# A four-step turn of the attention result on TensorE against one block transpose on VectorE, with one rectification in sixteen on ScalarE

## The reference

```python
x = x + attn(xn) + moe(xn)
# attn: 8 heads, 2 channels each for queries and keys, 16 for values
scores = einsum("bmhd,bnhd->bhmn", q, k) / sqrt(2)
scores = where(scores >= 0, scores, 0.2 * scores)
beta = softmax(scores)
out = gamma * einsum("bhmn,bnhd->bmhd", beta, v) + xn
# moe: 16 experts (1 zero, 1 copy, 2 constant, 12 MLP of 128 -> 512 -> 128), top 2, capacity 1024 slots each
```

## Time and profile before

| | us |
|---|---|
| median of 3 runs (976.41 to 978.05) | 977.33 |
| the profiled execution | 976.61 |
| its span | 974.8 |
| DVE, L1030, 512 rectifications | 610.7 busy, 1.229 each |
| ACT, L636, 512 exponentials | 523.3 busy, 1.024 each |
| ACT, L628, 32 copies of the result | 18.6 busy, 0.580 each |
| DVE, L1016 and L1011, 32 each | 13.3 and 7.9 busy |
| POOL, L400, 32 additions | 23.5 busy, 0.735 each |

### The profile page before, as it was taken

How to read it: one execution, slowest core, us unless ns; L and a number is a source line. 1 busy time by engine, 2 the same in 40 slices (tenths; PEclk the granted TensorE clock), 3 DMA queues, 4 the chain that set the end, 5 groups by cost and what they waited for, 6 DMA issues and landing times.

```text
span 974.8 us, 19803 instructions
## 1 busy us (share of the span) xinstructions
PE 883.5 (91%) x7619; PEld 365.8 (38%) x7620; DVE 744.3 (76%) x851; ACT 716.5 (74%) x859; POOL 581.7 (60%) x574
## 2 busy tenths in 40 slices
PE   0688249999999999999999989999999999999997
PEld 0444102333333333867767723333333333333332
DVE  6698889999999995001011089999999999999996
ACT  0689878888888887454454468888888888888886
POOL 3355137776676662999999015647566574665770
PEclk9999659999999999999999989999999999999999
DMA  8723100101100011242342210010011002002100
GB/s 228 269 65 72 31 27 30 44 30 36 39 25 28 18 52 58 68 135 92 110 135 78 80 43 26 22 49 20 26 32 39 23 21 64 24 13 62 31 7 22
DMA packets 48163, 55.34 MB, mean 57 GB/s; under 512 B 10714, under 2 KB 35122, under 8 KB 48080
## 3 DMA queue, kind: packets, MB, share of 16 engines
q1 hardware_dynamic: 38464, 44.10, 14.8%
q0 software_dynamic: 8192, 9.37, 3.3%
q10 hardware_dynamic: 1424, 0.76, 0.3%
HBM read 31.58 MB, written 30.02 MB: 63 GB/s over the span
## 4 chain that ended last, share of the span: by engine, by line
PE 77%; ACT 9%; DVE 6%; issue 4%; DMA 1%; SPq 1%; POOLq 0%; ACTq 0%; DVEq 0%
PE ps L765 26%; PE ps L745 15%; PE ps L735 13%; PE ps L825 8%; PE ps L817 8%; ACT pr L636 4%; PE ps L775 3%; ACT ot L628 2%; DVE xn L897 1%; SPq L248 1%; PE ps L695 1%; PE ps L806 1%; ACT y L614 1%; DMA y<-in_x 1%; ACT va L592 1%
## 5 line engine op out<-in xcount | busy, mean ns | idle before, releaser
L1030 DVE TENSOR_SCALAR ps<-ps 128x1024 f32<-128x1024 f32 x512 | 610.7, 1229 | 20.9 <-PE ps L735 6.6
L636 ACT ACTIVATE pr<-ps 128x1024 f32<-128x1024 f32 x512 | 523.3, 1024 | 111.5 <-PE ps L745 101.0
L765 PE MATMUL ps<-pr,vp 128*32 128x256 f32 x4096 | 327.7, 392 | 0.3
L745 PE MATMUL ps<-q,kz 64*128 64x512 bf16 x1024 | 201.7, 391 | 9.2 <-DVE ps L1030 9.1
L735 PE MATMUL ps<-q,kz 62*128 62x512 bf16 x1024 | 199.9, 387 | 7.7 <-DMA q<-parts_dram 1.7
L445 POOL DMA_INDIRECT xs<-eout,idxs x128 | 129.0, 1008 | 108.7 <-ACT pr L636 78.5
L430 POOL DMA_INDIRECT disp<-xn,idx x128 | 125.6, 981 | 47.1 <-issue 35.8
L1042 DVE TENSOR_TENSOR pr<-ps,parts 128x1024 f32<-128x1024 f32 x12 | 14.7, 1225 | 166.1 <-PE ps L825 166.1
L745 PEld LDWEIGHTS ps<-q,kz 64*128 64x128 bf16 x1024 | 49.2, 93 | 222.0 <-DVE ps L1030 117.2
L765 PEld LDWEIGHTS ps<-pr,vp 128*32 128x32 f32 x4096 | 81.2, 108 | 108.1 <-issue 91.3
L663 ACT ACTIVATE pr<-ps,b1s 128x512 f32<-128x512 f32 x96 | 66.0, 687 | 48.8 <-PE ps L817 48.8
(11 more groups left out here) (120 smaller groups left out, 618.6 us busy)
## 6 DMA issues: line engine op xcount, KB each, us to landing
disp<-pr SPq DMA_DIRECT2D x12, 512.0 KB, 4.9
eout<-pr SPq DMA_DIRECT2D x12, 512.0 KB, 2.9
y<-in_x SPq DMA_DIRECT2D x8, 512.0 KB, 8.2
out<-y SPq DMA_DIRECT2D x8, 512.0 KB
w<-in_w1t SPq DMA_DIRECT2D x12, 256.0 KB, 3.1
w<-in_w2t SPq DMA_DIRECT2D x12, 256.0 KB, 3.3
xs<-disp SPq DMA_DIRECT2D x6, 512.0 KB, 4.8
pr<-disp SPq DMA_DIRECT2D x6, 512.0 KB, 4.8
```

The costliest lines, as they stand in the source:

```text
L636: act.activation(pr[:, c % BUFS, 2 * pair:2 * pair + 2, :], ring[i % RING], ACT.Exp, scale=SLOPE).then_inc(S["exps"], 1)
L745: last = pe.matmul(ring[i % RING][:, k, :], kz[r:r + TILE, hg, pair, kc * P:(kc + 1) * P], q2[r:r + TILE, hg, qh * HALF:(qh + 1) * HALF], ...
L765: last = pe.matmul(acc[p % 2][32 * g:32 * g + 32, cols], vp[:, hg, kc, g, :], pr[:, c % BUFS, g % PAIRS * 2 + g // PAIRS, cols], start=(kc ...
L1030: dve.tensor_scalar(s, s, 0.0, 1.0 / SLOPE - 1.0, ALU.max, ALU.mult).then_inc(S["relu"], 1)
```

## The change

The result of a pass is no longer turned by PE. DVE transposes `acc` into `ot` by one instruction, which transposes each 32 x 32 block on its own. Since each head has a band of 32 partitions, afterwards partition 32g + r holds, for head g, the queries whose number modulo 32 is r, 16 of them, each with 16 values and its denominator in 32 columns. DVE then takes the reciprocal from SBUF. The product moves to POOL (`quotient`), and its result `att` still has heads on partition bands, so SP moves it by 16 DMAs per pass (`spread`) into `moved`, where each partition is one token, and POOL adds that to `y`. Each DMA has 32 partitions x 4 runs of 64 bytes.

In addition unit 9 of every pass is rectified by ACT (`rectify`), in place in PSUM, between exponentials 7 and 8.

```diff
-EVAC = 4
-TURN = 6
-DENOM = 12
-FINISH = 13
+TURN = 5
+PARTS = 1
+BLOCK = 32
+BY_ACT = 9
...
@@ SP
+            def spread(p):
+                sp.wait_ge(S["att_rdy"], p + 1)
+                wait_done(sp, "y_att", p - 1)
+                for g in range(HG):
+                    rows = att[BLOCK * g:BLOCK * g + BLOCK, p % 2, :, :].rearrange("q (t r) d -> q t r d", r=P // BLOCK)
+                    for r in range(P // BLOCK):
+                        sp.dma_start(moved[BLOCK * r:BLOCK * r + BLOCK, p % 2, :, g, :], rows[:, :, r, :]
+                                     ).then_inc(S[f"spread{p % 2}"], 16)
...
+            for p in range(BH * NPB):
+                operands_in(p)
+                if p > 1:
+                    spread(p - 2)
...
             sp.wait_ge(S["pv"], BH * NPB * TB)
+            spread(BH * NPB - 2)
             load_expert(1, 1)
+            spread(BH * NPB - 1)
...
+            spread(B * NPB - 1)
+            store_sequence(B - 1)
@@ POOL
+            def quotient(p):
+                pool.wait_ge(S["rg_rdy"], p + 1)
+                wait_done(pool, f"spread{p % 2}", 16 * HG * GT * (p // 2))
+                rows = ot[:, p % 2, :].rearrange("p (q c) -> p q c", c=BLOCK)
+                pool.tensor_tensor(att[:, p % 2, :, :], rows[:, :, 0:DV],
+                                   rg[:, p % 2, :].unsqueeze(2).broadcast_to([P, HALF // BLOCK, DV]), ALU.mult
+                                   ).then_inc(S["att_rdy"], 1)
...
@@ ACT
-            def evacuate(p):
-                act.wait_ge(S["pv"], TB * (p + 1))
-                wait_done(act, "o_rdy", p - 1)
-                act.copy(ot[:, p % 2, :], acc[p % 2]).then_inc(S["acc_evac"], 1)
+            def rectify(i):
+                act.wait_ge(S["s1"], i + 1)
+                s = ring[i % RING]
+                act.activation(s, s, ACT.Relu, scale=1.0 / SLOPE - 1.0).then_inc(S["relu_act"], 1)
...
+                    if (i + 1) % UP == BY_ACT:
+                        rectify(i + 1)
                     exponentials(i)
@@ PE
-                    if 0 <= i % UP - TURN < GT and i > first + UP:
-                        turn(i // UP - 1, i % UP - TURN)
...
-                for t in range(GT):
-                    turn(end // UP - 1, t)
...
                     if n == 2:
-                        pe.wait_ge(S["att_rdy"], NPB * BH)
+                        pe.wait_ge(S["turned"], NPB * BH)
@@ DVE
+            def turn(p, part):
+                if part == 0:
+                    dve.wait_ge(S["pv"], TB * (p + 1))
+                    wait_done(dve, "att_rdy", p - 1)
+                cols = slice(part * HALF // PARTS, (part + 1) * HALF // PARTS)
+                last = dve.transpose(ot[:, p % 2, cols], acc[p % 2][:, cols])
+                if part == PARTS - 1:
+                    last.then_inc(S["turned"], 1)
...
+                    if 0 <= i % UP - TURN < PARTS and i > first + UP:
+                        turn(i // UP - 1, i % UP - TURN)
+                    if i % UP == TURN + PARTS and i > first + UP:
+                        denominators(i // UP - 1)
+                    if i % UP == BY_ACT:
+                        continue
```

More of the change, by code:

```diff
@@ L199, in build @@
                  "qz_init weighted gate_rdy row_step route max_rdy off_rdy reset_rdy r_exp cnt_rdy pos_rdy ztile init_rdy kz_init "
-                 "ld0 ld1 vp_rdy s1 relu s2 exps pv acc_evac o_rdy rg_rdy att_rdy y_att "
+                 "ld0 ld1 vp_rdy s1 relu relu_act s2 exps pv turned rg_rdy att_rdy spread0 spread1 y_att "
                  "scat staged pool_step carry "
@@ L309, in store_sequence, with operands_in @@
                              y[:, bass.ts(s, TB), :]).then_inc(S["final"], 16)
[L312 to L315, removed]
+            def spread(p):
[6 more added lines that the diff above has]
+                                     ).then_inc(S[f"spread{p % 2}"], 16)
+            def operands_in(p):
+                if p % NPB == 0 and p > 0:
+                    load_operands(p // NPB, 1)
+                if p % NPB == NQ and p // NPB + 1 < B:
+                    load_operands(p // NPB + 1, 0)
+            for hg in range(NHG):
+                load_operands(0, hg)
+            for p in range(BH * NPB):
+                operands_in(p)
+                if p > 1:
+                    spread(p - 2)
             sp.wait_ge(S["scat"], 16 * GS)
@@ L341, in _ @@
                 store_expert(E_MLP - 2 + u)
[L343 to L349, removed]
+            for p in range(BH * NPB, B * NPB):
+                operands_in(p)
+                if p > BH * NPB + 1:
+                    spread(p - 2)
+                if p % NPB == 0 and p > BH * NPB:
+                    for s in STORES[p // NPB - BH - 1]:
+                        store_sequence(s)
+            spread(B * NPB - 2)
+            for s in STORES[B - BH - 1][:-1]:
                 store_sequence(s)
+            spread(B * NPB - 1)
+            store_sequence(B - 1)
             sp.wait_ge(S["final"], 16 * B)
@@ L741, in shifted @@
                 p, hg, qh, kc, pair = unit_of(i)
-                pe.wait_ge(S["relu"], i + 1)
+                if i % UP == BY_ACT:
+                    pe.wait_ge(S["relu_act"], i // UP + 1)
+                else:
+                    pe.wait_ge(S["relu"], i + 1 - (i + UP - BY_ACT) // UP)
                 for k in range(2):
@@ L761, in values @@
                     pe.wait_ge(S["vp_rdy"], p // NQ + 1)
-                    wait_done(pe, "att_rdy", p - 1)
+                    wait_done(pe, "turned", p - 1)
                 for g in range(HG):
@@ L1022, in attention @@
                 for i in range(first, end):
-                    done = i // UP - 1 if i > first + UP else None
-                    if done is not None and i % UP == DENOM:
-                        denominators(done)
-                    if done is not None and i % UP == FINISH:
-                        finish(done)
+                    if 0 <= i % UP - TURN < PARTS and i > first + UP:
+                        turn(i // UP - 1, i % UP - TURN)
+                    if i % UP == TURN + PARTS and i > first + UP:
+                        denominators(i // UP - 1)
+                    if i % UP == BY_ACT:
+                        continue
                     dve.wait_ge(S["s1"], i + 1)
@@ L1030, in attention @@
                     dve.tensor_scalar(s, s, 0.0, 1.0 / SLOPE - 1.0, ALU.max, ALU.mult).then_inc(S["relu"], 1)
+                for part in range(PARTS):
+                    turn(end // UP - 1, part)
                 denominators(end // UP - 1)
-                finish(end // UP - 1)
             attention(0, BH)
```

46 lines of the change are left out of this document (18 added, 28 removed).

## The result

The changed kernel takes 1000.15 us (median of 4 runs, 998.95 to 1000.82) against 977.68 before in the same series: a ratio of 1.023, 95% interval 1.0215 to 1.0247. It is slower by 22.5 us. The forecast was 986.1, slower by 8.8, with a range that ended at 1004. The sign was right, the time lies inside the range, and the size was off by more than a factor of two.

The account below looks back on a forecast made before the run. The prediction took a TensorE and ScalarE loop of 1.20 us a unit as the bound. Passes +1.8, between stages -0.9 and tail +7.9 sum to +8.8: 985.4 from 976.6 profiled, median 986.1, range 978 to 1004.

Parts of the forecast that it names:

- The bound: Kernel before: a loop of 1.20 us a unit through TensorE and ScalarE, not VectorE, sets the pace.
- ScalarE's rectification: In the loop, between exponentials 7 and 8: exponential 8 starts 0.55 to 0.73 us late, taken as 0.60.
- VectorE's lateness: At unit 6 of a pass: VectorE, with transpose and reciprocal, needs 4.36 us where 4.12 is due, 0.24 late.
- Sum +0.02: A pass: -0.82 us for removed transposes and copy, +0.24 on VectorE, +0.60 on ScalarE; times 30 is +0.6.
- Rival 1: In a pass, the block transpose costs as 1024 columns, 0.77 us late in place of 0.24: +16, 1002; chance 0.18.
- rival 2: VectorE was the bound, so a pass drops 0.83 us: 959, or about 968 with ScalarE's 0.60 half hidden; chance 0.12.
- rival 4: In a pass, transpose 0.33 and ScalarE 0.55 make -0.27 us; -1.4 in all, no tellable change; chance 0.06.
- the price of an issue: SyncE's 16 transfers of a pass: 0.35 us each to issue plus 0.04 between two, 6.2 us in all.
- +7.9: Tail at the kernel's end: 14.55 us in place of 6.6, including fifteen issues of 0.39 (5.85).
- -0.9: Between the stages: -1.2 us as the experts start at once, +0.3 for the later load of expert 1.
- Cover: In the passes: SyncE's transfers have a whole pass to run beside; if that is gone, everything paces at SP.
- Rival 3: SP paces the passes: at 1.86 us an issue, 16 are 30 us a pass, adding over 300 us; chance 0.02.

Follow-up runs that it names:

- e1: The changed kernel with unit 9 rectified by VectorE again, so ScalarE runs only exponentials: 982.5 us, 1.0065 of the kernel before.
- e13: The kernel of e10 with the reciprocal taken before rectification 13 in place of 6, run in a second series: 963.5 us, 0.987 of the kernel before.
- e4: The changed kernel with each partition's 256 bytes moved in one run in place of four of 64, values landing in wrong places: 997.8 us.
- e9: The changed kernel with the product sent to DRAM by one transfer first and the 16 transfers per pass reading from there: 1010.7 us.
- e10: The changed kernel without ScalarE's rectification, the product moved through DRAM by five transfers in place of 16: 964.6 us, 0.987 of the kernel before.
- e5: The changed kernel with ten of the last result's 16 transfers issued by ScalarE and six by SyncE: 994.6 us, 1.0177 of the kernel before.
- e3: The changed kernel with SyncE's list between the stages reordered, the load of expert 1 first: 990.5 us.

## Why the prediction was right or wrong

**The bound was right.** A loop of 2.40 us for two units through TensorE and ScalarE. e1 shows it from one side (VectorE takes a sixteenth rectification and the pass gets shorter), and the 0.55 us of idle TensorE behind exponential 8 from the other.

**The terms of a pass were right.** Transpose 0.60 to the next start, measured 0.63. ScalarE's rectification 0.60, measured 0.58. VectorE's lateness 0.24, of which e1 leaves 0.2 over the bare loop and the pass shown above 0.23. Sum +0.02, measured -0.02. How VectorE's 0.24 was split, 0.60 from the transpose and 0.23 from the reciprocal against one slack, isn't borne out: e13 has the same passes without the 0.23. Rival 1, a transpose at the price of 1024 columns, is out, and so are rival 2, VectorE as the bound (its sum has a slip: 18.65 to 17.8 is 0.85, not 0.83), and rival 4, a pass 0.27 shorter.

**The rule on relu.** The Trainium skill, "ScalarE: Activation LUTs", rules for kernel authors, says to put it on VectorE, for speed per element, and its figure is for bf16. For this shape in four-byte values in PSUM that reason doesn't hold: 1.02 us on ScalarE (the L668 row) against 1.23 on VectorE. Its advice does, for another reason: ScalarE's operations are in the loop that sets the pace, and e1, with the rectification on VectorE, has passes 0.58 shorter.

**The step that failed is the price of an issue: "A transfer of 128 short runs (b1s, 16 bytes each) takes 0.35 to issue; I add 0.04 between two, so 16 take 6.2 us".** It measured 0.60 and 0.64, so 16 take 10.2, and 10.7 and 11.2 at the two ends. I chose a row by its number of runs, and e4 shows that this doesn't set the price. The trace of before had a row with both ends in SBUF, the eight small transfers into `kz` at the start, and I had not read it:

```profile
L256 SPq DMA_DIRECT2D kz<-rowones x8: 577/589/1617, 15.7 to 21.3; - x8
```

0.589, close to what was measured. That both have their ends in SBUF doesn't explain it, since e9 pays 0.599 from DRAM; but a price of 0.6 for a small transfer stood in the trace, as did the 0.624 of the second weight load (256 KB). The spread around the forecast took an issue to 0.45 at most, so the error was in the bounds too.

**It entered three times.** In the tail, fifteen steps of 0.68 in place of 0.39 are +4.3. Also in the tail, the last result's transfers stand behind those of the one before, 3.8 us (978.74 to 982.52). The prediction called the tail "laid bare" and began the issues at once. By its own price that would have held: the 32 issues from 960.16, at 0.39 each, end at about 973 (an estimate), before the product is ready. So this wait comes from the price too. Together with landings 0.4 shorter, +7.9 became +15.4. Between the stages the load of expert 1 went out at 394.4 in place of 389.0. That is 5.9 us of stall for which I had written 0.3, and then half the clock for some 6 us, which I had no term for: -0.9 became +7.5. POOL's rounds, which I had ending about 14 us later, ended 23.7 later (559.4), still beside the experts.

**Cover held where I named it.** Inside the passes the spread takes up half of SyncE's time (10.3 of 20 us) and the passes came out level. Rival 3, SyncE pacing the passes, was out by a factor of two.

## What to carry to other kernels

A step that is moved off the busy engines onto a queue is free only while something runs beside it. Work out the last one, and the one at each change of stage, as a bare sum, with all that the queue still has to issue ahead of it. Where no row is known to fit, bound the price of a DMA issue by the cheapest and the dearest row of small transfers (in the trace of before 0.25 and 0.59 us), not by the one that looks alike. Count the issues before the bytes: here five transfers by way of DRAM were cheaper than sixteen within SBUF. Before work is passed from the busiest engine to another, ask which of the two lies in the loop that sets the pace.

## What the runs showed of the hardware that was not expected

- An issue on SyncE cost 0.59 to 0.60 us for pieces of 8 KB in four forms (32 partitions by four runs of 64 bytes, from SBUF or from DRAM; 32 by 256 bytes; 128 by 64 bytes), 0.63 for 32 KB from SBUF to DRAM (e10), and 0.33 to 0.35 for 128 KB over 128 partitions in one run each. On ScalarE's queue the median was 0.622, against 0.601 on SyncE's for the same piece (e5). Two loads of one form cost 0.333 and 0.624, the second issued right behind the first.
- A block transpose of 128x512 four-byte values from PSUM takes VectorE 0.71 us, 0.63 to the next start, between its 256-column (0.33) and 1024-column operations (1.13).
- ScalarE rectifies 128x1024 in place in PSUM in 1.02 us, as long as it takes for an exponential into SBUF.
- After 5.9 us without work TensorE was granted 0.59 of its clock over 399 to 407 us, 0.50 up to 405; with the idle time taken away (e3), the experts ran at 1.00.
- In one series the kernel before took 1090 us in place of 977, and a kernel that is 1.3% faster elsewhere was 0.4% slower there. That kernel's passes were uneven and its granted clock lower in the attention stages (0.88 from 200 to 400 us). The record gives this series the same chip number as an earlier one with 976.7 us, so it isn't shown to belong to the chip. What set it off was not tried.
